# P times V of a cross attention: 32-column products on four column groups of TensorE in place of 128-column products

## The reference, cut to what matters

```python
qh = _split_heads(q @ Wq + bq)
kh = _split_heads(k @ Wk + bk)
vh = _split_heads(v @ Wv + bv)
logits = jnp.einsum('bhqd,bhkd->bhqk', qh, kh) / jnp.sqrt(jnp.asarray(DEPTH, dtype=qh.dtype))
logits = logits + mask * -1000000000.0
attn = jax.nn.softmax(logits, axis=-1)
out = jnp.einsum('bhqk,bhkd->bhqd', attn, vh)
out = out.transpose(0, 2, 1, 3).reshape(q.shape[0], -1, D)
return out @ Wo + bo
```

## Time and profile before

| what | value |
|---|---|
| median of 3 runs | 2039.79 us (2039.04 to 2040.78) |
| profiled execution, its own time | 2034.94 us |
| its span, first to last instruction | 2033.2 us |
| mean granted clock of TensorE | 0.981 |
| busy: TensorE, its weight loads, VectorE, ScalarE, GpSimd | 94%, 66%, 91%, 83%, 24% |
| one interval of the loop (892.7 to 1002.9 us) | 110.2 us |

### The profile page before, as it was taken

How to read it: one execution, slowest core, us unless ns; L and a number is a source line. 1 busy time by engine, 2 the same in 40 slices (tenths; PEclk the granted TensorE clock), 3 DMA queues, 4 the chain that set the end, 5 groups by cost and what they waited for, 6 DMA issues and landing times. The chain is left out here.

```text
span 2033.2 us, 37605 instructions
## 1 busy us (share of the span) xinstructions
PE 1902.7 (94%) x11661; PEld 1350.1 (66%) x11676; DVE 1851.3 (91%) x2320; ACT 1682.3 (83%) x4617; POOL 494.9 (24%) x392
## 2 busy tenths in 40 slices
PE   7998999999999999999999999999999999668799
PEld 5576776767676666767676767666676767466444
DVE  1546999999999999999999999999999999999788
ACT  3458989898989889898989898888989898867484
POOL 1001214131414223141314142422314131201013
PEclk9999999999999999999999999999999999788899
DMA  9522333333342333333333334233333333420214
GB/s 295 213 82 89 79 93 79 92 81 96 72 114 65 83 98 73 93 83 92 77 91 82 98 72 114 62 84 93 80 93 83 91 78 88 95 84 11 73 42 145
DMA packets 93396, 188.55 MB, mean 93 GB/s; under 512 B 18768, under 2 KB 39904, under 8 KB 88160
## 3 DMA queue, kind: packets, MB, share of 16 engines
q1 hardware_dynamic: 78448, 133.32, 20.9%
q0 software_dynamic: 14832, 54.01, 14.1%
HBM read 116.12 MB, written 17.18 MB: 66 GB/s over the span
## 5 line engine op out<-in xcount | busy, mean ns | idle before, releaser
L1443 ACT ACTIVATE dA<-dt,A_sb 128x124 f32<-128x124 f32 x2048 | 617.0, 391 | 11.3 <-DVE dt L1770 10.1
L1820 DVE TENSOR_TENSOR_SCAN hb<-dA,hb 128x2048 f32<-128x2048 f32 x118 | 522.4, 4427 | 8.1 <-ACT dA L1443 4.3
L992 PE MATMUL bank<-ctxT,wk_sb 128*128 128x256 f32 x2048 | 461.6, 383 | 13.4 <-ACT ctxT L1259 11.4
L1003 PE MATMUL bank<-wv_sb,ctxT 128*128 128x512 f32 x1024 | 465.2, 595 | 2.3 <-ACT ctxT L1259 2.3
L992 PEld LDWEIGHTS bank<-ctxT,wk_sb 128*128 128x128 f32 x2048 | 382.6, 191 | 77.2 <-ACT ctxT L1259 18.2
L1003 PEld LDWEIGHTS bank<-wv_sb,ctxT 128*128 128x128 f32 x1024 | 186.6, 191 | 188.6 <-issue 185.1
L1545 POOL DMA_DIRECT2D hb<-hb x103 | 93.3, 906 | 862.5 <-DVE hb L1826 846.6
L1815 DVE TENSOR_TENSOR hb<-u,BC 128x2048 f32<-128x2048 f32 x118 | 270.4, 2292 | 5.7 <-DVE u L1782 2.6
L1826 DVE TENSOR_TENSOR hb<-hb,BC 128x2048 f32<-128x2048 f32 x117 | 268.2, 2292 | 1.5
L1096 PE MATMUL bank<-xn2T,win_sb 128*128 128x128 f32 x2048 | 236.8, 277 | 0.7 <-ACT xn2T L1358 0.7
L1096 PEld LDWEIGHTS bank<-xn2T,win_sb 128*128 128x128 f32 x2048 | 234.1, 193 | 4.5 <-issue 2.4
(11 more groups left out here) (167 smaller groups left out, 2582.2 us busy)
## 6 DMA issues: line engine op xcount, KB each, us to landing
hb<-hb POOLq DMA_DIRECT2D x103, 512.0 KB, 4.8
ctx_sb<-in_ctx_dram SPq DMA_DIRECT2D x64, 512.0 KB, 3.7
BC<-bcd_dram SPq DMA_DIRECT2D x32, 1024.0 KB, 7.0
maskb<-in_mask_Bx1x1xS_fk_dram SPq DMA_DIRECT2D x64, 128.5 KB, 3.4
wstage<-in_L_ffn_w_dram SPq DMA_DIRECT2D x4, 2048.0 KB, 11.7
x_sb<-in_x_dram SPq DMA_DIRECT2D x16, 256.0 KB, 3.5
win_sb<-in_L_attn_in_proj_w_dram SPq DMA_DIRECT2D x1, 4096.0 KB, 25.2
bo_sb<-bias_dram SPq DMA_DIRECT2D x64, 64.0 KB, 2.1
```

Source lines behind the costliest of these rows:

```text
L992: last = pe.matmul(bank[6 + j][:, (m % 2) * KF:(m % 2 + 1) * KF], wk_sb[:, c, m * P:(m + 1) * P], ctxT[:, c, :], start=(c == 0), stop=(c = ...
L1003: last = pe.matmul(bank[h][:], ctxT[:, c, h * P:(h + 1) * P], wv_sb[:, c, :], start=(c == 0), stop=(c == DC - 1))
L1443: last = act.activation(dA[:, c % 2, n * BT:(n + 1) * BT, 1:], dt[:, c, :].rearrange("p (b s) -> p b s", s=S)[:, :, 1:], ACT.Exp, scale=A_ ...
L1820: ins = dve.tensor_tensor_scan(flat, dA[:, c % 2].rearrange("p n s -> p (n s)"), flat, 0.0, ALU.mult, ALU.add)
```

## The change

weigh_values goes through m, h and j: 32 products, each of the 32 columns of V of one head by the 32 columns of the transposed P of the same head, written to partitions 32j to 32j+31 of `bank[4]`, that is to column group j of TensorE. The result has only the wanted blocks, at column m x 32, and ScalarE takes it out in one copy of 128 partitions by 4 x 32 elements. `o_copied` counts one per batch element instead of four. The number and place of all other instructions stay.

```diff
@@ scores
-                    wait(pe, o_copied, HC * g)
+                    wait(pe, o_copied, g)
@@ weigh_values, TensorE
                     for m in range(DC):
                         for h in range(2):
-                            last = pe.matmul(bank[4][:, m * P:(m + 1) * P], V[:, h, m * P:(m + 1) * P],
-                                             PT[:, h, m, :], start=(h == 0), stop=(h == 1))
+                            for j in range(HC):
+                                dims = slice(m * P + j * DEPTH, m * P + (j + 1) * DEPTH)
+                                last = pe.matmul(bank[4][j * DEPTH:(j + 1) * DEPTH, m * S:(m + 1) * S],
+                                                 V[:, h, dims], PT[:, h, m, j * S:(j + 1) * S],
+                                                 start=(h == 0), stop=(h == 1))
                     last.then_inc(o_psum, 1)
@@ wo_product
-                    pe.wait_ge(o_copied, HC * BT * (t + 1))
+                    pe.wait_ge(o_copied, BT * (t + 1))
@@ weigh_values, ScalarE
-                    for j in range(HC):
-                        rows = slice(j * DEPTH, (j + 1) * DEPTH)
-                        act.copy(oT[rows, :, b * S:(b + 1) * S],
-                                 bank[4][rows, :].rearrange("p (m q) -> p m q", m=DC)[:, :, j * S:(j + 1) * S]
-                                 ).then_inc(o_copied, 1)
+                    act.copy(oT[:, :, b * S:(b + 1) * S],
+                             bank[4][:, 0:DC * S].rearrange("p (m q) -> p m q", m=DC)).then_inc(o_copied, 1)
```

## The result

| what | before | after |
|---|---|---|
| median | 2039.41 us (2037.44 to 2040.78, 4 runs) | 2020.68 us (2018.77 to 2022.96, 4 runs) |
| ratio of the medians | | 0.9909, 95% interval 0.9892 to 0.9927 |
| profiled execution, its own time, span | 2034.94, 2033.2 us | 2018.77, 2017.0 us |
| mean granted clock of TensorE | 0.981 | 0.979 |

The change makes the kernel 18.7 us faster. The forecast of 2027.1 us has the right sign; the time lies 6.4 us under it and 0.3 us under the low end of its range.

A forecast was written before the change was run, and what follows sets the result against it. TensorE was taken to bound the first intervals and VectorE to pace the loop. Savings of 3.9 + 1.8 + 6.5 + 0.5 = 12.7 us from the median of 2039.8 gave 2027.1 us, range 2021 to 2036.

The forecast's parts named there:

- element 0: First batch element, in interval 0: its saving ends in a 3.66 us wait for the context DMA, counted as nothing.
- elements 1 to 4: Interval 0 and first element of interval 1: bound by TensorE, saving 4 x 0.98 = 3.9 us.
- element 5 (to 7): Interval 1: TensorE's 0.98 and ScalarE's 0.8 us both shorten VectorE's 2.16 us wait for exponentials at element 5, 1.8 us.
- interval 2: Counted as one of 13 loop-like intervals, each saving 0.5 us of VectorE's wait for the exponentials.
- loop: ScalarE's shorter queue cuts VectorE's 0.70 us wait to some 0.2: 0.5 us by 13 intervals, 6.5 us with interval 2.
- interval 15 and rest: In interval 15 VectorE's 0.52 us wait for the scores goes, 0.5 us; the tail was given nothing.
- What reaches the end: Four steps of end-to-end saving: elements 0 to 4, element 5, the loop, interval 15; 3.9 + 1.8 + 6.5 + 0.5 us.
- The signs named for the scores of elements 4 and 8: Scores of element 4 (126.44) should start 2.9 us earlier, those of element 8 (233.29) 5.7 us earlier.
- the instructions don't arrive in time: Rival at P times V: supply of 128 array instructions lags, TensorE loses 2.1 us per element, some 2115 us; chance 0.05.
- threshold of 2.4 us: P times V's 64 passes make the kernel slower only above about 2.4 us, when the loop's idle TensorE time is used up.
- Nothing in the loop: Rival: ScalarE is late for another reason than its queue, VectorE's 0.70 us wait stays, 2034 us; chance 0.12.
- the 8 us forecast: Sign in the loop: TensorE idle near 8 us per interval after the change.

The follow-up runs named there:

- r1: Kernel before with the new 32-column products but still four copies of the result; 2030.38 us, ratio 0.9954 to the kernel before.
- r2: Kernel before with the old products but one copy, so three of four heads get wrong values; 2029.65 us, ratio 0.9954 to the kernel before.
- r0: The changed kernel measured again on another occasion; 2023.19 us, ratio 0.9925 to the kernel before.
- r4: The whole change from element 8 on, code before for elements 0 to 7; 2030.29 us, ratio 0.9964 to the kernel before.
- r5: Changed kernel with the loop over column groups outermost, sixteen passes in a row to one group; 2036.67 us, ratio 0.9996 to the kernel before.
- r10: Changed kernel with the 64 passes of P times V issued twice; 2024.89 us, ratio 0.9932 to the kernel before.
- r11: Kernel before with one more VectorE product per Mamba tile, 1.08 us per interval; 2051.37 us, ratio 1.0060 to the kernel before.
- r9: Changed kernel without the last of VectorE's three convolution taps; 2023.32 us, ratio 0.9929 to the kernel before.
- r8: Kernel before without the last of VectorE's three convolution taps; 2048.69 us, ratio 1.0053 to the kernel before.
- r6: Kernel before with the eight steps at L1764 moved from VectorE to ScalarE; 2056.81 us, ratio 1.0088 to the kernel before.
- r7: Changed kernel with the eight steps at L1764 moved from VectorE to ScalarE; 2042.55 us, ratio 1.0032 to the kernel before.

## Why the prediction was wrong where it was

**The mechanism held where it was worked out.** TensorE's saving was forecast at 0.98 us per element and is 1.00; P times V takes 0.69 us to the next group and 0.09 more at the entry, 0.79 in all where 0.81 was written. One copy takes 0.27 us for 0.28. The column groups run beside each other as the scores' rows said. VectorE's wait at L1710 went from 0.70 to 0.17, for a forecast of 0.2. The interval of the loop is 109.63 us for 109.7, VectorE's busy time 107.3 for 107.2.

**The terms of the sum.** For the measured side I take means over the profiled executions in which a stretch is as before and as after (two to six of each, of the kernels whose edit does not reach that stretch), since single ones scatter.

| term | forecast | measured | from |
|---|---|---|---|
| element 0 | 0 | 1.2 | 28.1 to 26.9; not the change's work, see below |
| elements 1 to 4 | 3.9 | 4.3 | 93.5 to 89.2 |
| element 5 (to 7) | 1.8 | 2.4 | 84.2 to 81.8; 2.0 row by row |
| interval 2 | 0.5 | 0.3 | 109.4 to 109.1 |
| loop | 6.0 | 6.4 | 1322.8 to 1316.3; by the median interval 6.8 |
| interval 15 and rest | 0.5 | 1.7 | 360.9 to 359.3, scatter of 2 us; 1.6 of it is shown below |
| sum | 12.7 | 16.3 | |

The failed step is the last of the four under "What reaches the end": **interval 15 at 0.5 us**. It measures 1.6. I read one wait there and overlooked another one of 0.70 us at L1770. The row of before, then the same instruction after:

```profile
1707.99 1.30 DVE L1770 SCALAR_TENSOR_TENSOR dt<-dt,xpad 128x512 f32<-128x512 f32 x2 [0.70 <-ACT xpad L1420]
```

```profile
1693.76 1.29 DVE L1770 SCALAR_TENSOR_TENSOR dt<-dt,xpad 128x512 f32<-128x512 f32 x2
```

It is a wait for ScalarE, but what shortens it is TensorE: it goes with the products alone (r1) and not with the copy alone (r2). VectorE gains 0.79 us there, 0.60 at the L1697 of the earlier trace rows and 0.24 at two small waits of L1756, 1.6 us together, in the changed kernel (after and r0) as in r4, and the same in r1.

Element 5 was undersized by a little. Beside the 2.16 us of the earlier trace rows, the wait at L1710 is 0.12 us after (too short for a bracket), 1.09 with the products alone and 1.21 with the copy alone:

```profile
183.95 0.18 DVE L1710 RECIPROCAL soft<-soft 128x4 f32<-128x4 f32 x1
```

```profile
187.72 0.18 DVE L1712 RECIPROCAL soft<-soft 128x4 f32<-128x4 f32 x1 [1.09 <-ACT Pr L1299]
```

```profile
192.08 0.18 DVE L1707 RECIPROCAL soft<-soft 128x4 f32<-128x4 f32 x1 [1.21 <-ACT Pr L1296]
```

Both savings lie on this path as the prediction says, 1.1 and 1.0 us, 2.0 together for 1.8. The 2.4 of the table has scatter in it: r4 waits 0.72 us more for ScalarE in interval 1.

Element 0 came as forecast, at nothing. TensorE reaches the wait for the context 20.4 us after VectorE's first L1697 in every kernel with the products of the change and 21.3 us in every one with the old, so it saves 0.90 us; but the wait ends when the DMA lands, at 58.2 to 61.3 us in all kernels and whatever the form. What is left of the stretch takes 1.59 us where the clock is full and up to 2.50 where it stands at half. The row after, for the 59.10 of the earlier trace rows:

```profile
58.34 0.66 PE L958 MATMUL bank<-idf,ctx_sb 128*128 128x128 f32 x4 [3.24 <-DMA ctx_sb<-in_ctx_dram]
```

The pair of profiles has 2.2 us there, by chance of landing and clock. The signs named for the scores of elements 4 and 8, 2.9 and 5.7 us earlier, therefore came as 5.0 and 9.6: 1.7 us of both is this chance, and by element 8 TensorE has also run further ahead of VectorE, which is 7.9 us earlier there.

The rest of the miss is how the sum was set against the runs, and in part luck. The terms without element 0's are 15.1 us; taken from the median that was shown they give 2024.7 us. r0 measured 2023.19, which lies inside the range, and the executions of the result 2020.68, which lies 0.3 us outside it. The kernel before, measured five times in this study, has medians of 2037.55 to 2039.41, all under the 2039.79 on which the forecast was built, and its single executions spread from 2034.87 to 2042.73. For the low end of the range I had allowed 2 us for that scatter and taken no mis-sized term with it; 4 us would have been the rows' own measure, since the profiled execution already lay 4.9 us under the median.

**What was right for a wrong reason.** The rival "the instructions don't arrive in time" did not come: 64 loads and 64 matmuls went in within 0.57 us. But the reason for its threshold of 2.4 us, and the remark that a slower TensorE would first use its own idle time, are refuted by r5: at 1.94 us per element the loop's gain is already gone, and TensorE's idle time absorbed nothing in front of the scores. "Nothing in the loop" is refuted by r2.

**Left out: the granted clock.** In the loop of before the clock is full throughout. After, it falls six times to half for 3.4 us, each time within 3 us after TensorE had waited: four times for P (1.1 us), once for Q (1.9) and once for ln_out. This last is the row of 1114.90 to 1118.30 above, which has 0.50, that is 1.2 of 2.4 GHz, and before it stands

```profile
1114.16 0.63 PE L1092 MATMUL bank<-idf,ln_out 128*128 128x128 f32 x4 [2.49 <-ACT ln_out L1304]
```

So what TensorE gained partly goes into a slower clock. The cost was small: r0 has four such stretches and the shortest loop of all, 1315.0 us, and r10, in which TensorE is busier and the clock never falls in the loop, has 1315.6. After the stretch shown VectorE lost 1.7 us against r0, all of it in front of L1756, whose rows wait for ScalarE's tap; ScalarE had waited 2.15 us for TensorE's products of L1099 (0.73 in r0):

```profile
1126.54 3.61 DVE L1756 SCALAR_TENSOR_TENSOR xs<-xpad,convw,xs 128x128 f32<-128x128 f32 x12 [0.87 <-ACT xs L1377]
```

At 1220.95, 24 us after the next fall began, it lost another 0.5 at L1710; that this belongs to the fall is not shown. The two make 2.2 of the 2.7 us by which the loop of after is longer than r0's. TensorE's idle time per interval is not the 8 us forecast (redone, 3.9 + 3.9 - 0.5 is 7.3): 109.63 - 104.94 = 4.7 us in this interval, with a stretch at half clock in it, 5.8 us on the mean of ten intervals in r0, and 6.4 to 6.5 in those intervals of r0's loop in which the clock stays full. So the clock explains part of the difference and not all.

## What to carry to other kernels

Ask of each engine that idles whether its idle time lies in front of the instruction that the bounding engine waits for; if not, it is no reserve: in r5 0.15 us more per element there, 0.6 per interval, made the interval 0.5 us longer than with the copy alone (110.22 for 109.73). A wait of the bounding engine that lasts the same in every round, also when the bounding engine has more to do (r11), may be part of the round: here it went with work taken out of the other's queue, four small copies made one, and that half of the change, which looked like a by-product, brought nearly the whole gain of the loop. To find the bound, add a known piece of work to one engine at a time: that gave clean answers here, while taking work away uncovered other waits. But added work tells what more would cost and not what less would bring: r9 took 1.6 us per interval off VectorE and gained nothing.

## What the runs showed of the hardware that I had not expected

- Matmuls with 32 columns of weights and 32 moving columns start 9.0 ns apart when neighbours in program order go to different column groups (64 passes over 0.567 us; 128 passes over 1.100 us in r10, 8.7 ns), and 27.2 ns apart on average when sixteen in a row go to the same one (r5, 64 over 1.716 us; 31 to 32 ns within a group). The Trainium skill ("TensorE: Matmul & The Clock Gate", "Wait — 56ns, not 53.3ns?") says that starts never come closer than about 25 ns. The trace agrees only within one column group; across groups it does not.
- Each weight load of 32 columns has a record of 110 ns and yet they follow each other at 8.6 ns on average (64 over 0.54 us): loads of different column groups run beside each other as the matmuls do.
- One copy of 128 partitions takes 267 ns, and one of 32 partitions with the same 128 elements 1.09 / 4 = 272: a copy's price here goes by its elements per partition, not by how many partitions it fills.
- Where VectorE had less to do, a gap opened once per interval of most of the loop at the scores (L1697), with no releaser in the trace: 0.3 to 1.2 us between the instruction and the reading of its sums in r8 and r9, and 0.3 to 1.2 us before the instruction in r6 and r7. What it waits for stays open.
